# Attention's sums of exponentials, one head (128x512) at a time instead of two or four heads at once

## The reference

```python
xt = jnp.transpose(x, (0, 2, 1))                    # B, T=512, D=256
qh = (xt @ Wq.T).reshape(B, T, NH, dk).transpose(0, 2, 1, 3)
scores = scale * jnp.einsum('bhqd,bhkd->bhqk', qh, qh)
logits = (scores * cmask + (1.0 - cmask) * NEG) * rmask
attn = jax.nn.softmax(logits, axis=-1)              # exp(l - max) / sum of exp
ctx = jnp.einsum('bhqk,bhkd->bhqd', attn, qh)
out = (ctx reshaped) @ Wo.T
x = x + ffn(out)                                    # 8 experts, top 2, and a shared expert
```

## Time and profile before

| | |
|---|---|
| median of 3 runs | 2060.32 us (2059.29 to 2061.53) |
| profiled execution | 2059.99 us, its span 2058.2 us |
| PE busy | 1922.2 us, 93% of the span |
| DVE busy | 1082.7 us, 53% |
| ACT busy | 709.4 us, 34% |
| POOL busy | 620.0 us, 30% |
| granted TensorE clock, mean | 0.964 |

### The profile page before, as it was taken

One profiled execution on the slowest core, in us unless ns is written; L12 is line 12 of the kernel. 1 busy time (PEld: TensorE's weight loads), 2 busy tenths in 40 slices (PEclk: granted clock), 3 DMA queues, 4 the chain that ended last, 5 costly groups with the idle time before them and its releaser, 6 DMA issues. The chain is left out here.

```text
span 2058.2 us, 30150 instructions
## 1 busy us (share of the span) xinstructions
PE 1922.2 (93%) x10324; PEld 1416.7 (69%) x10325; DVE 1082.7 (53%) x1723; ACT 709.4 (34%) x1276; POOL 620.0 (30%) x444
## 2 busy tenths in 40 slices
PE   4999999999999869899999999979999999999995
PEld 2444444444444347799999999868888888888874
DVE  3788878887888548443444433343423323242334
ACT  1566666666666623232333332231010101011000
POOL 3556566666665526211111111100101001010101
PEclk6899999999999969999999999989999999999998
DMA  7776767676765063422333232162302112130204
GB/s 125 111 115 100 111 96 130 101 108 98 128 90 73 21 226 97 150 91 100 124 124 111 83 115 82 67 182 73 102 21 82 41 61 66 36 102 0 93 26 143
DMA packets 117831, 195.83 MB, mean 95 GB/s; under 512 B 11264, under 2 KB 43008, under 8 KB 117776
## 3 DMA queue, kind: packets, MB, share of 16 engines
q1 hardware_dynamic: 106736, 158.94, 34.4%
q0 software_dynamic: 11040, 36.18, 6.1%
HBM read 100.68 MB, written 43.25 MB: 70 GB/s over the span
## 5 line engine op out<-in xcount | busy, mean ns | idle before, releaser
L420 DVE TENSOR_REDUCE maxcol<-ps_m 128x1 f32<-128x512 f32 x512 | 336.9, 681 | 138.5 <-PE ps_m L562 133.4
L337 ACT ACTIVATE e<-ps_e 128x512 f32<-128x512 f32 x512 | 297.3, 596 | 186.5 <-PE ps_e L557 185.7
L148 POOL TENSOR_TENSOR e<-e 128x2048 f32<-128x2048 f32 x64 | 225.6, 3524 | 179.0 <-ACT e L337 178.9
L1384 DVE TENSOR_TENSOR s_h_f<-s_silu,s_ps_u 128x512 f32<-128x512 f32 x77 | 52.9, 688 | 393.5 <-PE s_ps_u L1456 344.0
L562 PE MATMUL ps_m<-kside,qside 97*128 97x512 f32 x512 | 224.3, 443 | 34.7 <-DVE maxcol L420 19.1
L1326 POOL DMA_INDIRECT s_chosen<-routed,s_slot_now x64 | 61.6, 962 | 620.9 <-DVE s_total L1430 609.6
L557 PE MATMUL ps_e<-qside,kside 98*128 98x512 f32 x512 | 236.8, 465 | 3.3 <-ACT e L337 2.1
L557 PEld LDWEIGHTS ps_e<-qside,kside 98*128 98x128 f32 x512 | 96.8, 190 | 191.8 <-ACT e L337 158.7
L1352 ACT ACTIVATE s_silu<-s_ps_g 128x512 f32<-128x512 f32 x77 | 46.0, 598 | 528.8 <-PE s_ps_g L1456 521.3
L1053 DVE TENSOR_TENSOR e_h_f<-e_silu,e_ps_h 128x256 f32<-128x256 f32 (+1 forms) x108 | 45.2, 418 | 250.1 <-ACT e_silu L894 250.1
L562 PEld LDWEIGHTS ps_m<-kside,qside 97*128 97x128 f32 x512 | 101.1, 197 | 80.6 <-DVE maxcol L420 54.6
(11 more groups left out here) (233 smaller groups left out, 4189.0 us busy)
## 6 DMA issues: line engine op xcount, KB each, us to landing
routed<-e_y SPq DMA_DIRECT2D x36, 512.0 KB, 2.8
kside<-q_hi SPq DMA_DIRECT2D x64, 256.0 KB
qside<-qm_hi SPq DMA_DIRECT2D x64, 256.0 KB
x_f<-in_x SPq DMA_DIRECT2D x16, 512.0 KB, 3.5
kside<-q_lo SPq DMA_DIRECT2D x32, 256.0 KB
qside<-qm_lo SPq DMA_DIRECT2D x32, 256.0 KB
attn<-xo SPq DMA_DIRECT2D x32, 256.0 KB, 3.4
keep_rows<-attn SPq DMA_DIRECT2D x8, 1024.0 KB, 5.6
```

The lines of the kernel that those rows point to most:

```text
L148: eng.tensor_tensor(into, into, e[k + 1][:, heads, :], ALU.add).then_inc(done, 1)
L337: act.activation(e[kb][:, g, :], ps_e[g % 2][:, :], ACT.Exp, scale=SCALE).then_inc(e_done, 1)
L420: dve.reduce_max(maxcol[par][:, g * KB + kb:g * KB + kb + 1], ps_m[g % 2][:, :], AX.X).then_inc(max_done, 1)
L1384: dve.tensor_tensor(h_f[:], silu[:], ps_u[:], ALU.mult).then_inc(h_done, 1)
```

## The change

`add_pair` no longer issues its sum as one instruction over a slice of heads, but one instruction of 128x512 for each head, and only the last of them raises the semaphore. The three calls pass a range of heads instead of a slice.

```diff
         eng.wait_ge(e_done, (KB * u + k + 2) * HG)
         eng.wait_ge(num_mm, KB * u + k + 1)
-        into = e[k][:, heads, :]
-        eng.tensor_tensor(into, into, e[k + 1][:, heads, :], ALU.add).then_inc(done, 1)
+        for g in heads:
+            into = e[k][:, g, :]
+            last = eng.tensor_tensor(into, into, e[k + 1][:, g, :], ALU.add)
+        last.then_inc(done, 1)
...
-                add_pair(pool, u - 1, 1, slice(HG // 2, HG), pair_pool)
+                add_pair(pool, u - 1, 1, range(HG // 2, HG), pair_pool)
...
-                add_pair(pool, u, 0, slice(0, HG), pair_pool)
+                add_pair(pool, u, 0, range(HG), pair_pool)
...
-                        add_pair(dve, u - 1, 1, slice(0, HG // 2), pair_dve)
+                        add_pair(dve, u - 1, 1, range(HG // 2), pair_dve)
```

## The result

| | before | changed |
|---|---|---|
| median of 6 runs | 2060.68 us (2059.29 to 2062.07) | 2070.93 us (2067.59 to 2080.48) |
| ratio | 1 | 1.0056, 95% interval 1.0035 to 1.0078 |
| profiled execution | 2059.99, span 2058.2 | 2072.25, span 2070.5 |

Forecast were 2066.5 us and a loss of 0.3%. The loss is 10 us by the medians, some 12 by the profiled executions and by the ratio, and not 6: right in sign and place, half in size. The six runs of the changed kernel lie 13 us apart and these six of the kernel before 3; over the 22 of the kernel before that stand beside the first experiments it is 9 us (2055.5 to 2064.4, one more execution of 4994.65 us left aside).

The account below looks back on a forecast made before the run. TensorE was taken to set attention's pace, VectorE following closely. 2059.99 - 5.3 - 1.1 + 12.6 = 2066.2, plus 0.3 for the median: 2066.5 us; own range 2061 to 2071, over the cases 2053 to 2072.

Parts of the forecast that it names:

- What bounds attention: In attention TensorE sets the pace, VectorE close behind; behind `c_f` six reductions in 3.84 us pace TensorE.
- The plain lengths: Divided sums last longer: GpSimd's pair 0 +0.41 us, its part of pair 1 +0.15, VectorE's sums +0.09; taken as 0.
- `c_f` at the seam: VectorE's `c_f` gets in between the halves of GpSimd's part of pair 1, ending 1.1 us early without mask rows.
- rival C: No change: `c_f` doesn't get in between the two halves, all ends 0.10 to 0.15 us later; 2063.0 us, chance 0.16.
- rival D: Slower by more: `c_f` gets in only where mask rows follow; 2073.3 us, chance 0.08.
- `c_lo` ahead of `row_neg`: At ends with mask rows GpSimd's `c_lo` goes before VectorE's `row_neg`, by 0.02 to 0.12 us, so reductions start later.
- rival B: Faster: `row_neg` gets in before `c_lo`, so only the gains stay; 2053.9 us, chance 0.17.
- Gains at ends without mask rows: At 15 ends without mask rows `c_f` ends earlier, gaining 0.35 us each, 5.3 us together.
- The sum: 2059.99 - 5.3 - 1.1 + 12.6 = 2066.2 us; with the median 0.3 above the profiled execution, 2066.5 us, 0.3% slower.
- 12 x 1.05 = 12.6 us lost: At 12 ends with mask rows TensorE's `ps_m` starts 1.05 us later, and nothing gives it back.
- bare sums: VectorE's two divided sums with nothing hiding their extra 0.09 us, 32 times: 2.9 us, kept only for the range.

Follow-up runs that it names:

- the added wait: The changed kernel, with `c_lo` on GpSimd in steps with mask rows also waiting until `row_neg` is done: 2048.77 us, ratio 0.9936.

## Why the prediction was right or wrong

- **What bounds attention (right).** That VectorE's reductions pace TensorE behind each `c_f`, and that a delay of them is not given back, held to a tenth of a microsecond: 1.14 us per end for 1.05.
- **The plain lengths (right).** 5.01 for pair 0 and 2.52 for the part of pair 1 where nothing interferes, as worked out, and no time for either; VectorE's pair of sums 1.28 for 1.30. By the formula for one instruction in the Trainium skill (VectorE: DVE Perf Modes, The TRN2 errata), taken twice, the extra one would be 0.16 us, an estimate; the trace shows less, some 0.07 (1.28 for 1.216), since two in a row overlap by 0.08, and dividing the other two sums cost nothing measurable.
- **`c_f` at the seam (right), rival C and D out.** In the changed kernel each `c_f` that started between 143.62 and 636.68 us got in between the halves. At 123.35, where it came 1.41 us behind the first half's start, it missed the seam.
- **`c_lo` ahead of `row_neg` (right), rival B out.** A margin forecast as 0.02 to 0.12 us was decided the same way at every steady end; in the trace `c_lo` starts 0.12 to 0.18 us ahead of `row_neg` there. Had it fallen the other way, the change would have been a gain, as the added wait shows.
- **Gains at ends without mask rows (right, a third too small).** 0.48 us each for 0.35.
- **The sum (wrong): the step "12 x 1.05 = 12.6 us lost".** It counted the delay (measured: 13.7) as all that a longer idle time costs. At 1.86 us of idle time TensorE's clock then went down to half speed in 7 of 12 cases, 9.7 us in the profiled execution. With it the forecast would have been 2076 us by the same sum, with the larger gains at the other ends and in the first units 2073. The rows had it: `ps_m` at 107.93 took 0.79 us behind 3.98 of idle time, and I read only the idle time of that row. The earlier trace rows had it too: I took its clock for the full one, but it is 0.98, and the missing part is half speed from 62.0 to 72.2 and from 106.4 to 113.2 us. The range had no case for it either; beyond 2071 only rival D reached. It was also added up wrongly: gains of 0.1 to 0.6 us at 15 ends and up to 2.9 us of bare sums give 2063 to 2073 us, not 2061 to 2071. That the measured median, 2070.93, lies within both is luck, as the dips are no part of either.
- **The spread (open).** Why the changed kernel's runs differ so much (2067.6 to 2080.5) isn't shown. Dips that come at some ends and not at others would do it, but what is on record doesn't bear it out: the mean granted clock was 0.966 in the longest of the six and 0.965 in the shortest, and the kernel with the lengthened idle time, 9 dips in its profile, has its four runs within 1.2 us. What follows attention, the same in all kernels, lasted 1331.5 to 1338.1 us in the profiled executions, so part of the spread can lie there.

## What to carry to other kernels

Where two engines exclude each other on an instruction's whole length, its length is part of the schedule: cutting it in two lets the other engine in at the seam, and then one has to go through who is queued next on both sides, since the same cut saved 7 us at one kind of end and cost 21 at another. Move the short instruction that gets caught (here two mask rows of 0.4 us each) to a place where the other engine is idle before cutting anything. And price a longer idle time of TensorE with the spell of half speed that may follow it, not by its length alone: look in the trace of before for matmuls behind its longest waits.

## What the runs showed of the hardware

- An instruction of VectorE with two SBUF inputs, or a 1x512 cast or multiply-and-add in SBUF, and a GpSimd instruction that reads SBUF take turns whole; between two queued GpSimd instructions the waiting one of VectorE gets in, even when it has waited for only about 0.1 us (`c_f`: 0.76 us for 0.69 undisturbed). By the rule that GpSimd's cores go on to the next instruction each by itself (the Trainium skill, GPSIMD Engine Reference, Instruction dispatch) this could have failed; in the steady state it did not once.
- Behind idle times of 1.67 to 1.90 us TensorE went to half speed at many ends: 7 of 12 in the changed kernel, 8 of 12 with GpSimd's half alone divided, 10 of 12 with it divided only at ends with mask rows, 9 of 12 with the lengthened idle time. In the changed kernel it began 0.5 to 1.9 us behind the end of the idle time (276.31 to 278.1), with the lengthened idle time 0.9 to 2.3 us (280.80 to 282.1); it lasted 3.4 us each time, but for one of 6.8 us in the latter. Behind idle times of 0.67 to 0.84 us it did so in 1 of 60 (12 steady ends in each of five profiled kernels: before, the two other sums divided, `c_lo` behind the rows, the repeats, and divided only at ends without rows). So a shorter idle time makes a dip rare and not impossible, and what decides in the single case these runs don't tell.
- Repeating a matmul in such an idle time cost nothing that can be told (0.9995 where there was no dip to win) and kept the clock at 1.00 at all 12 steady ends of the profiled execution.
